# One transformer block on one core: the scatter moved ahead of a weight load, row turns moved inside a tile, key weights moved and scores made twice

## The reference, cut to what matters

```python
x = x + attention(layernorm(x))      # x: 1024 tokens x 256, f32; 16 heads of 16
x = x + experts(layernorm(x))

# attention
q, k, v = h @ Wq.T, h @ Wk.T, h @ Wv.T          # q and k rotated over the whole width of 256
k_feat, q_feat = elu(k) + 1, elu(q) + 1
mem_out = q_feat @ (k_feat^T v) / (q_feat . sum(k_feat))      # linear attention, per head
attn = softmax(q k^T / 4) v                                   # full attention, per head
out = (sigmoid(gate) * mem_out + (1 - sigmoid(gate)) * attn) @ Wo.T

# experts
logits = xf @ router_w.T                        # 8 experts
top 2 of 8, softmax over the two
y_e = (silu(xf @ gate_w[e].T) * (xf @ up_w[e].T)) @ down_w[e].T     # width 688
out = sum over the two chosen e of weight * y_e
```

## Time and profile before

| what | value |
|---|---|
| runs | 439.78, 443.24, 442.66 us, median 442.66 |
| the profiled execution | 444.38 us, span 442.5 us |
| TensorE busy, granted clock | 403.9 us of the span, 0.96 |
| VectorE, ScalarE, GpSimd busy | 254.1, 206.5, 123.6 us |

### The profile page before, as it was taken

The page is one execution under the profiler, slowest core; times in us unless marked ns, Lnnn a source line. Parts: engine busy times, 40 slices in busy tenths (PEclk is TensorE's granted clock), DMA queues, the critical chain, the costliest instruction groups (busy, mean ns, idle before and its releaser), DMA issues.

```text
span 442.5 us, 6916 instructions
## 1 busy us (share of the span) xinstructions
PE 403.9 (91%) x2374; PEld 231.7 (52%) x2375; DVE 254.1 (57%) x511; ACT 206.5 (47%) x393; POOL 123.6 (28%) x122
## 2 busy tenths in 40 slices
PE   6897979999999999999997999889799999999891
PEld 2453744222222222422321234789689988997891
DVE  7499779878888887689797210656121331112130
ACT  4328736776767676566665796221111211121120
POOL 8016783140302012011035032018511112322312
PEclk9699769999999999999999899999799999999998
DMA  7126905547432608030032196416322121321332
GB/s 266 43 79 101 308 25 95 99 128 244 120 142 63 197 1 272 0 118 11 2 128 99 40 377 188 152 50 201 72 40 33 32 43 24 50 33 28 37 107 25
DMA packets 22876, 45.05 MB, mean 102 GB/s; under 512 B 4448, under 2 KB 15584, under 8 KB 22016
## 3 DMA queue, kind: packets, MB, share of 16 engines
q0 software_dynamic: 9216, 30.28, 24.0%
q1 hardware_dynamic: 13008, 13.74, 11.9%
q10 hardware_dynamic: 624, 0.66, 0.5%
HBM read 23.76 MB, written 15.59 MB: 89 GB/s over the span
## 4 chain that ended last, share of the span: by engine, by line
PE 74%; DVE 15%; issue 3%; DMA 2%; another core or an unknown queue 2%; ACT 2%; POOL 1%; DVEq 0%; POOLq 0%; ACTq 0%
PE psum L1360 71%; DVE mem L1071 8%; DMA mem<-weights 2%; ACT mem L891 1%; DVE mem L1136 1%; PE psum L1499 1%; PE psum L1630 1%; DVE mem L1249 1%; DMA mem<-x 1%; DVE mem L985 1%; POOL mem L586 0%; PE psum L1525 0%; DVE mem L1075 0%; PE psum L1412 0%
## 5 line engine op out<-in xcount | busy, mean ns | idle before, releaser
L1360 PE MATMUL psum<-mem 128*32 128x512 f32 (+15 forms) x2242 | 391.8, 409 | 24.6 <-DVE mem L1071 7.1
L1360 PEld LDWEIGHTS psum<-mem 128*128 128x128 f32 (+8 forms) x2242 | 217.1, 148 | 186.3 <-issue 81.2
L1071 DVE TENSOR_REDUCE mem<-psum 128x1 f32<-128x1024 f32 x128 | 152.1, 1219 | 32.3 <-PE psum L1360 29.9
L891 ACT ACTIVATE mem<-psum 128x512 f32<-128x512 f32 x256 | 137.6, 604 | 62.2 <-PE psum L1360 59.9
L1236 DVE COPY mem<-mem 128x3 f32<-128x3 f32 x18 | 3.3, 184 | 92.7 <-PE psum L1630 84.6
L908 ACT ACTIVATE mem<-psum 128x384 f32<-128x384 f32 (+3 forms) x32 | 15.0, 472 | 83.5 <-PE psum L1360 81.0
L722 POOL DMA_INDIRECT sum_d<-mem x17 | 26.6, 1562 | 80.0 <-ACT mem L916 60.3
L680 POOL DMA_DIRECT2D mem<-gate_up x21 | 15.3, 731 | 107.6 <-DMA mem<-mem 107.6
L916 ACT ACTIVATE mem<-psum,mem 128x256 f32<-128x256 f32 x18 | 8.5, 474 | 40.8 <-PE psum L1360 38.7
L1249 DVE TENSOR_TENSOR mem<-mem,psum 128x384 f32<-128x384 f32 (+3 forms) x32 | 15.5, 525 | 5.4 <-ACT mem L908 3.6
L698 POOL DMA_INDIRECT xg_d<-mem x16 | 15.7, 983 | 4.8 <-issue 4.8
(11 more groups left out here) (128 smaller groups left out, 199.0 us busy)
## 6 DMA issues: line engine op xcount, KB each, us to landing
xg_d<-mem POOLq DMA_DIRECT2D x8, 1036.0 KB, 9.6
mem<-gate_up POOLq DMA_DIRECT2D x8, 688.0 KB
mem<-gate_up POOLq DMA_DIRECT2D x8, 624.0 KB
mem<-down POOLq DMA_DIRECT2D x4, 1024.0 KB, 8.7
mem<-mem SPq DMA_DIRECT2D x54, 64.0 KB, 3.9
mem<-mem SPq DMA_DIRECT2D x18, 128.0 KB, 4.4
mem<-xg_d SPq DMA_DIRECT2D x16, 129.5 KB, 2.3
mem<-x SPq DMA_DIRECT2D x4, 256.0 KB, 3.2
```

The source lines that it names most:

```text
L891: nc.scalar.activation(prob[:, t % 8], psum[:, score_bank(n, t)], ACT.Exp, scale=HD ** -0.5).then_inc(exp_ready, 1)
L1071: V.tensor_reduce(mx[:, par, k:k + 1], banks(2 * (k % 2), 2), AX.X, ALU.max).then_inc(max_ready, 1)
L1360: return nc.tensor.matmul(*a, **k)
```

## The change

The diff, cut to its core.

```diff
-WAKE = 18
+WAKE = 24
-        LIN_STEP = [34, 36, 38, 40, 41, 42]
+        TURN_STEP, STATE_STEP, LIN_STEP = [13, 14, 15, 16], [19, 21, 23, 25], [30, 32, 35, 37, 39, 41]
+        LATE = E - ENDS - 1
         def downs(g):
-            last = GATED.index(DIRECT - 2)
-            start = GATED[g - 1] if g - 1 != last else DIRECT
-            return range(start, GATED[g] if g != last else DIRECT)
+            own = (LATE, GATED.index(DIRECT - 2))
+            start = GATED[g - 1] if g - 1 not in own else GATED[g]
+            return range(start, GATED[g] if g not in own else GATED[g + 1])
 # SyncE
             for i in range(4):
                 sp.dma_start(x[:, 2 * i:2 * i + 2, :], x_v[:, 2 * i:2 * i + 2, :]).then_inc(x_in[i], 16)
+                if i == 1:
+                    sp.dma_start(wqkv[:, 0], w_d[:, 0]).then_inc(w_in[0], 16)
 # GpSimd
-            pool.wait_ge(res_ready[0], 2)
-            other(1)
-            other(3)
+            pool.wait_ge(mid_ready[0], 1)
+            other(0)
+            pool.wait_ge(lo_ready[0], 3)
+            for i in range(1, 4):
+                other(i)
...
             pool.wait_ge(lg_ps, 2)
+            scatter(1)
             for to, src in gate_up_pieces(gu[:, E - 1], gu_d[:, E - 1]):
                 pool.dma_start(to, src).then_inc(gu_in, 16)
-            scatter(1)
 # ScalarE
-            act.wait_ge(x_in[0], 16)
-            act.dma_start(wqkv[:, 0], w_d[:, 0]).then_inc(w_in[0], 16)
             normalise(0)
             normalise(1)
+            act.wait_ge(w_in[0], 16)
+            nc.scalar.copy(w_turned[:, 0, 0].rearrange("p (q r j) -> p q j r", r=HD, j=4),
+                           wqkv[:, 0, 0].rearrange("p (q j r) -> p q j r", j=4, r=HD)).then_inc(w_turned_ready[0], 1)
...
             for j in range(4):
                 v_copy(j)
+            for i in range(len(LIN_TURN)):
+                turned_features(i)
             act.wait_ge(rope_0, 4)
-            act.wait_ge(rope_q1, 2)
+            act.wait_ge(rope_1, 4)
             for hf in range(2):
-                for i in (2 * hf, 2 * hf + 1):
-                    turned_features(i)
                 feature_parts(qfeat, exp_q, qT, hf)
...
             attention(act, steps)
+            nc.scalar.activation(silu_1, half_c[:, 0:1], ACT.Silu)
             osb_copy(UNITS - 1, 1)
-            turned_copy(1, 1)
-            tile_silu(0)
-            tile_silu(1)
+            tile_silu(0, 0)
+            turned_copy(1, 1)
+            tile_silu(0, 1)
+            tile_silu(1, 0)
+            tile_silu(1, 1)
...
             for g in range(3, len(GATED)):
-                tile_silu(g)
+                tile_silu(g, 0)
+                if GATED[g] <= DIRECT:
+                    tile_silu(g, 1)
                 for t in downs(g):
                     tile_weigh(t)
+                if GATED[g] > DIRECT:
+                    tile_silu(g, 1)
 # VectorE
-            V.tensor_copy(w_turned[:, 0].rearrange("p b (q r j) -> p (b q) j r", r=HD, j=4),
-                          wqkv[:, 0].rearrange("p b (q j r) -> p (b q) j r", j=4, r=HD)).then_inc(w_turned_ready[0], 1)
+            V.tensor_copy(w_turned[:, 0, 1].rearrange("p (q r j) -> p q j r", r=HD, j=4),
+                          wqkv[:, 0, 1].rearrange("p (q j r) -> p q j r", j=4, r=HD)).then_inc(w_turned_ready[0], 1)
...
             rest(0)
-            other(0)
+            gates()
             first_turn(1)
             low_part(0)
             rotated(1, 0).then_inc(rope_0, 1)
-            turns(1, 1).then_inc(rope_mul, 1)
+            turn(1, 1, 0)
             rest(1)
             first_turn(2)
+            rotated(2, 0).then_inc(rope_0, 1)
             low_part(1)
-            rotated(2, 0).then_inc(rope_0, 1)
+            rest(2)
+            turn(1, 1, 1).then_inc(rope_mul, 1)
+            low_part(2)
             turns(2, 1).then_inc(rope_mul, 1)
-            rest(2)
-            gates()
-            low_part(2)
-            other(2)
             first_turn(3)
...
-                if s == 29:
+                if s == 27:
                     mask_state()
...
             mix(UNITS - 1, NQ - 1, 1)
+            hidden_half(0, 0)
             xgT_copy(1)
             take_meta(1)
             for k in range(2):
                 add_x(1, k)
-                for n in (2 * k, 2 * k + 1):
-                    second_stats(1, n, last=n == 3)
-                if k == 0:
-                    hidden(0)
+            hidden_half(0, 1)
+            for n in range(4):
+                second_stats(1, n, last=n == 3)
             spreads(4, 8)
             xgT_copy(2)
+            hidden_half(1, 0)
             for n in range(4):
                 second_norm(1, 0, n)
+            hidden_half(1, 1)
             for n in range(4):
                 second_norm(1, 1, n)
-            hidden(1)
...
             for g in range(3, len(GATED)):
+                if g == LATE:
+                    hidden(g)
                 if g + 1 < len(GATED):
                     for n in rows_behind(g):
                         xgT_copy(n)
                         take_meta(n)
-                hidden(g)
+                if g != LATE:
+                    hidden(g)
 # TensorE
-            def score(i, t):
+            def score(i, t, again=0):
...
-                ins = mm(psum[:, 2 * (k % 2) + kh], qst[0:SROWS, u % 4, j, qb * P:(qb + 1) * P],
-                         kst[0:SROWS, u % NQ, j, cols(kh)], start=True, stop=True)
+                for _ in range(1 + again):
+                    ins = mm(psum[:, 2 * (k % 2) + kh], qst[0:SROWS, u % 4, j, qb * P:(qb + 1) * P],
+                             kst[0:SROWS, u % NQ, j, cols(kh)], start=True, stop=True)
...
             for s in range(LEAD):
-                score(0, s)
-                if s in (15, 16, 19, 20):
-                    lin_turn(*LIN_TURN[(15, 16, 19, 20).index(s)])
-                if s in (23, 24, 25, 26):
-                    lin_state((s - 23) // 2, (s - 23) % 2)
+                score(0, s, again=s not in TURN_STEP + STATE_STEP + LIN_STEP)
+                if s in TURN_STEP:
+                    lin_turn(*LIN_TURN[TURN_STEP.index(s)])
+                if s in STATE_STEP:
+                    lin_state(STATE_STEP.index(s) // 2, STATE_STEP.index(s) % 2)
...
             def turn_x(x):
                 pe.wait_ge(xg_in[x % 2], 16 * loads(x))
-                if x:
-                    pe.wait_ge(xgT_ready, x)
+                before = [n for n in range(x) if shared(ROWS_IN[n]) == shared(ROWS_IN[x])]
+                if before:
+                    pe.wait_ge(xgT_ready, before[-1] + 1)
...
             turn_o(UNITS - 1, 1)
-            gate_up(0, 1)
+            gate_up(0, 1, (0,))
             post(1, "combT", 1)
+            gate_up(0, 1, (1,))
             turn_x(1)
...
             gate_up(1, 1)
+            gate_up(2, 0, (0,))
             post(1, "xn2T", 2)
-            pe.wait_ge(xgT_ready, 3)
             post(1, "xn2T", 3)
-            gate_up(2, 0)
+            gate_up(2, 0, (1,))
             post(1, "logits", 0)
             gate_up(2, 1)
             post(1, "rank", 0)
...
             for g in range(3, len(GATED)):
-                for half in range(2):
-                    gate_up(g, half)
-                if g + 1 < len(GATED):
-                    for n in rows_behind(g):
+                gate_up(g, 0)
+                rows = rows_behind(g) if g + 1 < len(GATED) else ()
+                if g != LATE:
+                    for n in rows:
                         turn_x(n)
+                if GATED[g] <= DIRECT:
+                    gate_up(g, 1)
                 for t in downs(g):
+                    if t == GATED[LATE]:
+                        for n in rows:
+                            turn_x(n)
                     down(t)
+                if GATED[g] > DIRECT:
+                    gate_up(g, 1)
             down(NT - 1)
```

More of the change, by code:

```diff
@@ L219, in block_kernel @@
         row_i = keep(NMORE, dt=I32)
-        more_f = keep(1)
+        silu_1 = keep(1)
         more_i = keep(2, dt=I32)
@@ L917, in weigh, with tile_silu @@
                                             scale=weight_y[:, t:t + 1])
-            def tile_silu(g):
-                for half in range(2):
-                    act.wait_ge(gu_ps, 2 * g + half + 1)
-                    silu(half, wide(g)).then_inc(silu_ready, 1)
+            def tile_silu(g, half):
+                act.wait_ge(gu_ps, 2 * g + half + 1)
+                silu(half, wide(g)).then_inc(silu_ready, 1)
             def tile_weigh(t):
@@ L1003, in _, with turn @@
             dve.wait_ge(rope_in, 16)
-            def turns(i, b):
-                m, p = (tmp, tmp_odd)[i % 2], QK_BANK[i]
-                if i >= 2 and b:
-                    dve.wait_ge((rope_k1, rope_q1)[i % 2], 1)
-                elif i >= 2:
-                    dve.wait_ge(rope_0, i - 1)
-                c = cols(QK_IDX[i][1])
-                V.tensor_tensor(m[:, 2 * b], psum[:, p + b], rope[:, 0, c], ALU.mult)
```

(27 more changed lines are left out.)

18 lines of the change are left out of this document (8 added, 10 removed).

## The result

| | median | runs | ratio to the kernel before |
|---|---|---|---|
| before | 442.69 us | 439.78 to 443.24 | |
| after | 425.75 us | 424.02 to 427.58 | 0.962 [0.958, 0.966] |

What follows compares the result with a forecast made beforehand. TensorE, busy 91% of the span, was taken as the bound. Gains of 5.2, 1.2, 9.5 and 2.7 less 3.0 made 15.6 us off 444.38, so 428.8; going halfway to the median gave 428 us, range 423 to 437.

Steps and rivals of the forecast that it cites:

- first stage: Start of the kernel up to the first score: keys start 1.9 us sooner and run at the higher clock, 5.2 us together.
- transition: From attention's end through the scatter to tile M0: TensorE's waits and the low clock behind them go, 9.5 us.
- Signals in time: Rival, 13%: TensorE's late signal around the scatter's end does not recur, so 425 us.
- about 5 us sooner: Sign at the first reduce: the forecast is wrong if it does not come this much earlier.
- The clock's 3.3 us: Keys' eight records: at the higher granted clock they take half of 6.63 us.
- Lead: First reduce to first exp: making 30 of 44 scores twice holds the clock; 30.8 against 32.05 us, 1.2 us gained.
- the 3.0 taken back: Scatter's end: a late signal may recur and stop TensorE at tile 4, so 3 us of the gain are deducted.
- near 311.4: Tile 4: time in us of the recurring late signal, 2.9 us sooner than before, with TensorE arriving at 310.
- order of the turn, other work in hand: Tile 4: two of four parts of the late-signal loss counted as mended, so 3 us deducted, between nothing and 5.9.
- The scatter's start: Second half's scatter: no longer behind three load issues, it starts at 298.3, not 301.26; near 292 with earlier gains.
- End: Last tiles and output adds: waits of 0.79 and 1.71 go, last add 1.9 us sooner; together 2.7 us.
- the late parts: Around the scatter: TensorE's 2.96 us wait at tile 4 and 2.95 us of low clock behind it, both forecast to go.

Runs made afterwards that it cites:

- the second pair of traces: Unchanged repeats, traced side by side: the kernel before, 443.69 us in one run, and the changed kernel, 425.72 us, ratio 0.963.
- The trace with 0.82 us of stand: Changed kernel with expert 7's load ahead of the scatter again and the key weights behind x's third piece: 426.22 us, ratio 0.962.
- back part alone: Kernel before with only the changed transition and expert loop, the rotation's sums kept on GpSimd: 427.80 us, ratio 0.987.
- second comparison: Follow-up runs on one chip, kernel before at 442.83 us: both kernels repeated, the scatter's order alone on the kernel before, two edits to the changed kernel.
- first and third: Follow-up runs on two other chips, kernel before at 433.56 and 434.03 us: parts of the change undone; the changed kernel repeated in the later one, 423.09 us.

## Why the prediction was right, point by point

**The total** was right to 2.3 us of median, and some of that is luck: the first stage gave 1.6 us less than forecast, the transition 3.9 more, and 0.9 came from attention by chance. The median, 425.75, lies nearest to what the rival *Signals in time* gave (425), yet the signals were late; the time alone would have been read wrongly.

**First stage, 5.2 us forecast, 3.6 measured.** The keys started at 11.51, not 10.6, because I gave x's second half "over 1 us in hand" behind a quarter MB; it waited 1.76 us. By the forecast's own sign ("about 5 us sooner" for the first reduce) this is a miss: 3.6. The cause was as said, its size was not. The starts on record are 10.60 to 11.51 over the traces with the early load. The clock's 3.3 us came as 2.9 (6.63 to 3.70) in the result's trace, but is not certain: one trace of the changed kernel has 5.27. The sums on GpSimd gave nothing, as said. By the rule that the prediction weighed (the Trainium skill, "SBUF — State Buffer", Who interferes with whom), a VectorE operation with two inputs in SBUF should block such a sum or be blocked; here the sums met almost only products with one input in PSUM (four in 2.48 us beside two sums, two in 1.27 elsewhere), so the rule was hardly put to the test. The cast, 1.03 us in the earlier trace rows, took 0.64 in the changed kernel, again beside a GpSimd operation; it has one input, so it says nothing of a rule on two, as the forecast had it.

**Lead, 1.2 forecast, 1.6 measured** (3.6 in the second pair of traces, 1.0 to 1.8 by the kernel with single scores). The clock held at 1.00 in every trace with doubled scores. VectorE kept one wait over 1 us (1.20 at the last pairs), which "none of VectorE over 1 us" denied.

**Transition, 9.5 forecast, 10.4 measured; the 3.0 taken back was wrong.** I argued that a late signal that belongs to the scatter comes again and stops TensorE for 1.3 to 2 us. It came again, 2.2 and 3.0 us late, and stopped nothing. The step that failed is the time of the signal, "near 311.4". The projection's turn comes 6.1 us sooner in the changed kernel, so that is 305.3 there, behind the end of the scatter, with TensorE at tile 4 at 303.9. TensorE came at 302.7, not far off. But the turn of tile 4 stands before the second half of tile 3 now; it ended at 298.01, 3.7 us before the scatter did, and its signal came at 300.2, 5 us sooner than I had put it. The two parts that I had counted as mended, "order of the turn, other work in hand", were enough for all of it. The trace with 0.82 us of stand shows how near it was.

**The scatter's start was right by two errors.** It was forecast near 292 and came at 291.67. The logits came 0.8 us sooner than forecast (287.11, not 294.3 - 6.4 = 287.9), and from there I gave the scatter 4.0 us (298.3 - 294.3), 0.4 less than before, for leaving its place behind three issues of 0.7 us. It takes 4.4 in the kernels with the load ahead and 4.6 in those with the load behind. The earlier trace rows shows the scatter behind "issue", which reads like a queue that holds it; but the slots were ready at 300.6 and it started 0.65 us later, where the changed kernel, with a free queue, starts it 0.8 us after its slots (290.85 to 291.67). The 2.96 us at tile 4 went by the order of the turn and by the row of indirect DMAs that ends sooner.

**End, 2.7 forecast, 2.6 measured.** The bound by adds 4.1 us apart held.

**Where the gain depends on the chip.** The ratio is 0.962, 0.963 where TensorE's signals are late and 0.974 where they aren't; the intervals don't meet. Of 17 us, about 6 are there only where the kernel before is slower. The kernel before takes 8.8 us more on such a chip (442.83 against 434.03), the changed one 2.6 (425.72 against 423.09), nearly all of the latter in attention: 2.3 us between first exp and logits, at the first half's scatter, which the change doesn't touch. Not all of the 8.8 need be signals: the median granted clock of the kernel before is 0.962 there and 0.968 here, and (1 - clock) x span, an estimate of what the low clock costs, is 16.8 us against 13.8. Leaving out the late parts (2.96 and 2.95) the forecast's terms sum to 5.2 + 1.2 + 3.6 + 2.7 = 12.7; measured there, 10.9.

**What the parts are worth, on chips without late signals:** the order of tiles 0 to 2 3.5 us, the turns and last halves 7.8 us while the load stands behind the scatter, key weights 3.2, second scores 1 to 2, the scatter's order nothing or a loss of 1. They don't add up: transition and experts together gave 5.8 (back part alone), not 3.5 + 7.8. The excess is 5.5 us; the 3.50 of wait and the 3.4 of clock that came where the load stands behind the scatter and the turns are not moved would cover it. That is argued, not shown: the kernel with the turns undone and the load ahead was not run.

**Still open:** why signals are late in the result and the second comparison and not in the first and third, and whether that goes with the chip. No trace of the kernel before exists from the first or third, so its 6.5 us outside attention are the difference of times less 2.3, not read. Pacing the scatter's issues was not tried.

## What to carry to other kernels

Before a step is moved ahead on a queue, find the wait that ends last for it: "issue" before an instruction does not show that what stood ahead of it was holding it. Put the consumer's turn inside a tile, with half a tile of work behind it: that covered late rows, late signals and the clock fall behind them, and with the cut of the last tiles it was worth 7.8 us here, as long as the load stood behind the scatter. Undo each part on its own, on more than one chip: the same edit was worth 17 us in two comparisons and 11 in another.

## What the runs showed of the hardware

- During a row of indirect DMAs from GpSimd, semaphore signals of TensorE came up to 4.4 us after the end of the record in all six traces of the result and the second comparison; the eight traces of the first and third have none over 0.3 us. The last came 1.1 to 1.7 us after the row ended. A matmul's end is modelled in the trace, and the Trainium skill says the same and that the signal follows it ("Perfetto Trace Analysis", Tensor Engine Instruction); it gives no length for that step, and no run here shows what holds it.
- The same kernel (the one before), in the second comparison and the third, on two chips: 437.63 to 445.02 and 432.36 to 435.43 us.
- 24 equal matmuls on ones at the start of the program took 6.77 to 8.32 us, though the clock column reads 1.00 for all of them: the first are 0.43 us apart, the later ones 0.22, and the place of the step between them differs from trace to trace.
- In the first stage the keys ran at the upper level after pauses up to 0.9 us and partly at the lower after one of 1.4 us or more, in all fourteen traces.
- The fetches of tile M0's rows (four of 32 rows) landed 1.8 to 3.0 us after their issue where the 1.4 MB load was ahead of the scatter (one trace), and 4.2 to 5.9 us after it where the load ran beside them (seven traces, first and third comparison).
